# A two-layer graph attention kernel: its first stage laid out anew, and one carry in another form

## The reference

```python
xr = jnp.einsum('nd,rdf->rnf', x, W)
oi = xr[etype, dst]
oj = xr[etype, src]
alpha = jax.nn.leaky_relu(oi @ q + oj @ k, NEG_SLOPE)
m = jax.ops.segment_max(alpha, dst, num_segments=n_nodes)
e = jnp.exp(alpha - m[dst])
z = jax.ops.segment_sum(e, dst, num_segments=n_nodes)
a = e / (z[dst] + EPS)
msg = (a[:, :, None] * oj.reshape(-1, heads, out_ch)).reshape(-1, heads * out_ch)
out = jax.ops.segment_sum(msg, dst, num_segments=n_nodes) + b
# twice: h = elu(layer1(x)); x = layernorm(x + layer2(h))
```

## Time and profile before

| | us |
|---|---|
| median of 3 runs | 2490.14 (2489.93 to 2492.66) |
| the profiled execution | 2489.6 |
| its span, first to last instruction | 2488.0 |
| first stage (to the first dense product) | 122.97 |
| dense products of layer 1 (to the first edge step) | 575.75, to 698.72 |
| the rest | 1789.3 |

### The profile page before, as it was taken

One profiled execution on the slowest core, in us unless ns is written; L12 is line 12 of the kernel. 1 busy time (PEld: TensorE's weight loads), 2 busy tenths in 40 slices (PEclk: granted clock), 3 DMA queues, 4 the chain that ended last, 5 costly groups with the idle time before them and its releaser, 6 DMA issues.

```text
span 2488.0 us, 42686 instructions
## 1 busy us (share of the span) xinstructions
PE 2415.6 (97%) x10277; PEld 1677.5 (67%) x10277; DVE 1370.7 (55%) x2672; ACT 1051.6 (42%) x2973; POOL 1604.4 (64%) x1671
## 2 busy tenths in 40 slices
PE   6999999999989999999989999999997999999998
PEld 2755666666589999999976566665554555555554
DVE  8438566655588988888897443332331332333232
ACT  1111000000179999999975000000002566666664
POOL 1277777767367777777735766667723677777774
PEclk9899999999999999999999999999999999999999
DMA  8642333333279998989843222322226999999996
GB/s 298 192 128 61 89 102 104 101 78 78 61 272 328 322 315 309 326 308 326 301 163 106 69 85 82 92 81 75 75 62 181 340 336 348 334 340 344 340 332 236
DMA packets 164481, 505.17 MB, mean 203 GB/s; under 512 B 55800, under 2 KB 61473, under 8 KB 164132
## 3 DMA queue, kind: packets, MB, share of 16 engines
q0 software_dynamic: 95664, 354.41, 42.4%
q1 hardware_dynamic: 54449, 143.18, 17.8%
q10 hardware_dynamic: 14256, 6.14, 1.1%
HBM read 424.00 MB, written 79.54 MB: 202 GB/s over the span
## 4 chain that ended last, share of the span: by engine, by line
PE 91%; DMA 3%; POOL 2%; DVE 2%; issue 1%; DVEq 0%; ACT 0%; ACTq 0%; SPq 0%; POOLq 0%
PE banks L994 35%; PE banks L1036 23%; PE banks L1060 11%; PE banks L1056 11%; PE banks L879 3%; PE banks L710 3%; PE banks L902 1%; PE banks L897 1%; POOL q_fill L1435 1%; DMA big<-q_fill 1%; POOL big L1448 1%; PE banks L721 1%; PE banks L703 1%; POOL ring L1473 1%; DVE big L1649 1%
## 5 line engine op out<-in xcount | busy, mean ns | idle before, releaser
L1473 POOL DMA_INDIRECT ring<-xr_table,row_idx x704 | 666.7, 947 | 303.2 <-PE banks L1036 96.2
L1448 POOL DMA_INDIRECT big<-k_table,row_idx x700 | 683.1, 976 | 275.4 <-issue 203.6
L1252 ACT ACTIVATE work<-work,wE 128x125 f32<-128x125 f32 x1760 | 552.6, 388 | 36.7 <-DVE work L1954 22.4
L994 PE MATMUL banks<-work 128*125 128x384 f32 x1548 | 534.0, 488 | 0.0
L1036 PE MATMUL banks<-ring,work 128*125 128x193 f32 x2816 | 470.5, 327 | 7.6 <-DMA ring<-xr_table,row_idx 7.6
L1036 PEld LDWEIGHTS banks<-ring,work 128*125 128x125 f32 x2816 | 464.2, 187 | 7.8 <-issue 7.8
L1971 DVE TENSOR_TENSOR big<-big,banks 125x772 f32 x440 | 421.5, 958 | 64.9 <-PE banks L1036 57.7
L1825 DVE TENSOR_TENSOR ring<-ring,banks 125x384 f32<-125x384 f32 x330 | 182.2, 553 | 490.6 <-PE banks L994 489.2
L994 PEld LDWEIGHTS banks<-work 128*125 128x125 f32 x1548 | 283.4, 188 | 181.8 <-issue 0.6
L994 PE MATMUL banks<-big,work 128*125 128x384 f32 x1152 | 398.0, 487 | 0.0
L1274 ACT ACTIVATE work<-rel,wE 128x125 f32<-128x125 f32 x440 | 216.2, 491 | 234.5 <-PE banks L1060 225.4
(11 more groups left out here) (276 smaller groups left out, 2038.3 us busy)
## 6 DMA issues: line engine op xcount, KB each, us to landing
xr_table<-ring SPq DMA_DIRECT2D x75, 337.8 KB
xr_table<-ring SPq DMA_DIRECT2D x75, 336.9 KB
work<-in_L_gnn_W SPq DMA_DIRECT2D x36, 384.0 KB, 6.2
ring<-xr_table,row_idx POOLq DMA_INDIRECT x704, 5.0
big<-k_table,row_idx POOLq DMA_INDIRECT x700, 2.4
work<-in_x_turned SPq DMA_DIRECT2D x25, 375.0 KB, 5.3
out<-work SPq DMA_DIRECT2D x25, 336.0 KB
work<-in_x SPq DMA_DIRECT2D x23, 336.0 KB
```

The lines of the kernel that those rows point to most:

```text
L994: last = pe.matmul(bank[b][0:TN, 0:HALF], left_side(l, left, pair)[:, c, :], right_side(l, left, r)[:, c, :], start=(left in ("A11", "S1", ...
L1252: last = nc.scalar.activation(one_hots[l][:, slot, h, :], hot[:, slot, :], ACT.Copy, scale=wE[:, bass.ds(st, 1), h:h + 1].rearrange("p a b ...
L1448: nc.gpsimd.indirect_dma_start(k_at(l, st), None, ktab[l], bass.IndirectOffsetOnAxis(ap=row_idx[:, st:st + 1], axis=0)).then_inc(s["k_gath ...
L1473: nc.gpsimd.indirect_dma_start(row_slot(l, st % GS), None, xrtab[l], bass.IndirectOffsetOnAxis(ap=row_idx[:, st:st + 1], axis=0)).then_inc ...
```

## The change

1. **Loads.** q1 and k1 come as 24 contiguous numbers for each partition (`qk_rows`), and ACT copies them to `qkw`. Turned W1 is laid out to match, with 3 + 12 slots; the 12 new ones are the places in `work` where W1 of relations 2 and 1 goes later. SP no longer waits for slots until the 16th chunk. x tiles 0 to 9 come in between the last chunks, then tiles 20 to 24, W1 of relation 0, tiles 10 to 19, the rest of W1, and b1 last. The edge lists wait for 9 chunks on PE, the zero fill for two groups of x; it is read 12 times (3 for layer 2) from a 440-wide piece of `rel` that POOL clears.
2. **Counts.** Digits of 6 bits by shift and mask: 49 high, 64 low values. Ten rounds go with W1, seven with the first seven x groups. DVE's work on the edge lists stands behind the counts.
3. **x.** Tiles in 13 groups (`GROUPED`), ten of them pairs of tiles 0 to 19, then two, one and two. A pair is one product of 250 columns.
4. **Warming.** PE begins with 11 products of `iota_n` with itself.
5. **q carry of layer 1.** As in layer 2 before: one scan over `same` gives `q_first`, which is 1 up to the first change of node in a row, and the carry is a multiply-add on the scans already made. `sum_w(0)` stands between `q_ends` and `q_carries`.
6. **Spots.** The two turns of q move from units 3 and 4 of the third plain tile to units 0 and 2 of the fourth. The last `turn_k` and what follows it in the softmax stand later.

```diff
-    WSLOTS = 3
+    WSLOTS = 3 + 2 * DC
-    K_SPOTS = [[168, 171, 174, 186], [192, 194, 224, 227]]
-    ENDS_SPOT, CARRY_SPOT = [192, 230], [195, 233]
+    K_SPOTS = [[168, 171, 174, 193], [192, 194, 224, 227]]
+    ENDS_SPOT, CARRY_SPOT = [199, 230], [201, 233]
-    PASS_SPOTS = [[196, 198, 200, 202], [234]]
-    E_SPOTS = [[205, 207], [238]]
+    PASS_SPOTS = [[202, 203, 204, 205], [234]]
+    E_SPOTS = [[206, 208], [238]]
...
-            for n in range(WSLOTS):
+            for n in range(WT - ROOMS):
                 load_turned_w1(n)
+            for t in range(ROOMS):
+                load_turned_w1(WT - ROOMS + t)
+                load_room(t)
             for k in range(U):
-                load_turned_w1(WSLOTS + k)
...
+                    for c in range(DC):
+                        last = pe.matmul(out_, wsb[:, c, NQK - 2 * R * H:NQK], chunks[:, :, c, :],
+                                         start=(c == 0), stop=(c == DC - 1))
...
-                        if done < 3 * (n + 1) // 4:
+                        if n >= 2 and done < COUNTED_WITH_W * (n - 1) // (WT - 2):
...
+                    for u in range(FLATS):
+                        if done < HROUNDS:
+                            hist(done)
+                            done += 1
+                            if done == HROUNDS:
+                                hist_end()
+                        first_products(u)
+                        if u > 0:
+                            first_turn(u - 1)
+                        if u == COUNTS_AT + 3:
+                            turn_counts()
+                        if u == COUNTS_AT + 4:
+                            sum_counts()
+                    first_turn(FLATS - 1)
...
-                    meets = {0: {2: turn_rows}, 2: {3: turn_q_ends, 4: turn_q_carry}} if l == 0 else {}
+                    meets = {0: {2: turn_rows}, 3: {0: turn_q_ends, 2: turn_q_carry}} if l == 0 else {}
...
+                    for u in range(FLATS):
+                        if u == COUNTS_AT:
+                            act.wait_ge(cnt_ready, 1)
+                            act.dma_start(node_counts.rearrange("(a b) -> a b", a=HI), digit_counts).then_inc(counts_stored, 16)
+                        if u == COUNTS_AT + 1:
+                            act.wait_ge(counts_stored, 16)
+                            act.dma_start(counts, node_counts[0:N].rearrange("(t p) -> t p", p=TN)).then_inc(counts_loaded, 16)
+                        first_flat(u)
+                        if u > 0:
+                            first_nodes(u - 1)
...
             pool.wait_ge(pads_set, 1)
+            pool.wait_ge(LS[0]["qk_done"], 2 + WT // 2)
...
-            pool.wait_ge(zeros_set, 1)
+            pool.wait_ge(LS[0]["qk_done"], 2 + WT + 2)
...
                     for q in range(R * H):
-                        if l == 0:
-                            link(nc.vector.tensor_tensor_scan(qs[:, q, :], same[0:ROWS, :], raw[:, q, :], c_in[:, q:q + 1],
-                                                              ALU.mult, ALU.add))
-                        else:
-                            link(nc.vector.scalar_tensor_tensor(out=qs[:, q, :], in0=q_first, scalar=c_in[:, q:q + 1],
-                                                                in1=qs[:, q, :], op0=ALU.mult, op1=ALU.add))
+                        link(nc.vector.scalar_tensor_tensor(out=qs[:, q, :], in0=q_first, scalar=c_in[:, q:q + 1],
+                                                            in1=qs[:, q, :], op0=ALU.mult, op1=ALU.add))
```

253 lines of the change are left out of this document (130 added, 123 removed).

## The result

The changed kernel takes **2478.27 us** (median of 5 runs, 2475.89 to 2482.68) beside 2492.44 for the kernel before on the same chip (2489.93 to 2492.76): a ratio of 0.995, with a 95% interval of 0.9939 to 0.996. It is faster by some 14 us, as forecast in sign; the forecast was 2469 and its range 2460 to 2478. The median lies 0.3 us above that range and 9 above the forecast. The profiled execution took 2475.9 us, its span 2474.2.

What follows compares the result with a forecast made beforehand. PE, carrying 91% of the time to the end, bounds the kernel, so only an earlier start of its dense products pays: 20.5 + 0.7 = 21.2 us off the profiled 2489.6 gives 2468.4; median 0.5 higher, 2469, range 2460 to 2478.

Steps and rivals of the forecast that it cites:

- S: Time at which the count sums come in the first stage: forecast 91 us, 88.5 if the clock holds.
- the low clock between W1 and the groups: First stage: clock of 0.50 only near 47 to 53 us, for which 2.6 us were added.
- block products: Their start, behind the dense units and DVE's first x sums: 220.8 instead of 241.3, 20.5 us earlier; S + 129.8.
- The wait at the q ends: PE at the turn of the q ends: a 3.9 us wait where 0.3 stood, plus 1.4 for the clock.
- The carry: Layer 1's q carry on DVE by multiply-add: 0.77 us each, 9.2 instead of 15.8, 6.6 less.
- W1 is hidden behind DVE: First stage without slot gating: W1 chunks and ten x tiles land by 35 to 40 us, while DVE's tables set the pace.
- the forecast's own signs: Wrong if dense start lies past 102, the two-tile product isn't 2.6, or PE waits over 6 us in the dense stage.
- the counts' trip: Counts' round trip through HBM: 5.49 + 4.81 us, started at 75.4, back near 86, hidden with about 1 us of cover.
- Rival 2: First stage: counts' trip 3 to 5 us longer or rounds at 4 us, S 4 to 8 later: 2474 to 2478, chance 0.27.
- the first use of the tables: PE's first use of DVE's digit tables, after the fourth chunk of W1: near 13.5 us.
- the end of the dense stage: Last turn of k moved 7 products later: its 0.7 us wait goes; the 7.6 us to the first edge product stay.
- three gathers fewer: POOL's gathers beside DVE's new multiply-adds, 9 us: three fewer, 4 us of POOL, inside its pauses; sum unchanged.

Runs made afterwards that it cites:

- f1: The change with W1 of relations 2 and 1 held until the counts are back, ACT's table load ahead of q1 and k1, 17 warming products: 2469.93 us, ratio 0.9916.
- a0: The changed kernel run once more, nothing altered: 2480.61 us, ratio 0.9959 to the kernel before.
- a3: The change with layer 1's carry again by twelve scans, its output not the reference's: 2823.15 us beside 2843.7 for the kernel before, ratio 0.9917.
- f2: The kernel before with only layer 1's carry by multiply-add, second run: 2490.44 us, ratio 1.0001.
- e1: The change with SP again waiting on three W1 slots and PE waiting for each chunk by itself: 2485.58 us, ratio 0.9977.
- a1: The change with W1 of relations 1 and 2 and b1 held back until the counts are back: 2473.24 us, ratio 0.9933.
- a2: The change with the store of k of tiles 5 to 9 placed just behind the counts' store: 2479.88 us, ratio 0.9959.
- the ACT edit: ACT's digits copy, and with it its table load, moved ahead of its wait for q1 and k1; alone in the change, ratio 0.9939.
- g1: f1 with layer 1's spots as before the change: 2772.63 us beside 2787.0 for the kernel before, ratio 0.9947.
- b1: The change with ACT's digits copy and table load ahead of its wait for q1 and k1: 2831.3 us beside 2843.7 for the kernel before, ratio 0.9939.

## Why the prediction was right and wrong

**Right.** That an earlier start of the dense products is all that pays, and where the holes went. A group of a round, a pair and two turns takes 3.81 (3.9 forecast), a pair 2.64 (2.6), S to the dense start 5.3 (5.4), the low clock between W1 and the groups at 51 to 57 (47 to 53). From S on the chain came nearly as worked out: block products at S + 128.3 in the change and S + 128.8 in f1 (forecast S + 129.8). The 1.5 us are two small misses: the q ends were ready at S + 83.5 (84.2), and the 1.4 set aside for the clock behind them weren't spent, since it stayed at 1.00 from 181 to 190 us (in a0, after a wait of 3.19, it stood at 0.69 to 0.74 and the block products came at S + 130.6). The wait at the q ends was 2.2 instead of 3.9, in part because PE had already waited 1.0 at the turn of the edge rows, a wait that the forecast doesn't have. The carry took 9.42 (9.2), and a3 shows that it counted in full, f2 that it is worth nothing where PE comes later anyway. Taken back alone (e1), the slots are worth 5 to 7 us; the forecast had no price for them by themselves, only that W1 is hidden behind DVE with them gone; in the change no wait for W1 is left.

By the forecast's own signs it was wrong: the dense start lies past 102 (102.61), and PE waits over 6 us in the dense stage (1.0 + 2.2 + 1.4 + 1.4 + 0.3 = 6.3). The two-tile product is the 2.6.

**Wrong: the counts' trip.** The step read "started at 75.4, so the counts are back near 86 ... Cover of about 1 us". It took 15.65 us and PE stopped for 3.11 + 1.17. I had carried 5.49 + 4.81 over from the earlier trace rows, and that was the right price beside a full stream, which stood beside it there too; what I left out was the neighbour on its own queue. In the new order a store of k, 625 small pieces, is issued 1.0 us ahead of the counts (76.89 and 77.87), not 5.5 ahead (82.12 and 87.62). Rival 2 named the time (3 to 5 us longer) and gave the stream as its reason; a1 shows that the stream is needed, a2 that the neighbour is needed too. The stops are 4.3 of the 6.3 us by which S is late. Holding the stream back gave 5 to 7 us.

**Wrong: the first use of the tables.** 13.5 forecast, 15.94 and 16.91 measured, 13.76 to 14.03 where the clock was kept. I had let "the 11 warming products end near 6" and the first chunk begin by 8 or so without pricing the hole between them, although the forecast charges the clock behind every later hole. q1 and k1 landed at 7.4, then came ACT's table load of 1.28. Size: 2.4 us in the one profile, 3.4 in the other. Of the 2.4, some 0.9 are the later start of the first chunk (9.07, where 13.5 less four chunks of 1.34 makes 8.1) and 1.5 the clock (the four took 6.87 us, not 5.36); 2.0 of them were left at the last round. The rounds themselves kept their 3.5 us. Curing it gave the rest: 2473.2 to 2469.9, with the ACT edit, which alone brought no earlier first use.

**Wrong: the end of the dense stage.** The last turn of k waits no more (0.7, right), but the turn of the ends now waits 1.39 (its row stands above). It replaces that gain. What follows the first edge product is 1.3 us longer than in the profile of before (1790.6 against 1789.3); in f2, which changes nothing there, it is 1790.9, so that is no effect of the change but the difference between two profiles, as large as this.

**Was this the whole miss?** Nearly. f1, with both causes cured, gives 2469.93 against 2469 forecast, block products at 219.0 and the first edge product at 676.96 (forecast 220.8 and 677). That it comes within 1 us is in part luck, and no proof of every term: the start of the block products came 1.8 us better than forecast, the stretch to the first edge product 1.3 worse and what follows 1.5 worse. As for the chances: the case "2474 to 2478" stood at 0.27 and is the one that came, with S 6.3 us late (4 to 8 in that case) and half of its reason. A median 0.3 above its end means little beside executions from 2475.9 to 2482.7; what the case left out is the low clock behind the stop, 2.5 us in a0 and a2.

## What to carry to other kernels
Price a small transfer by its neighbours on its own queue, not only by the load of the DMA engines: a store of many small pieces 1 to 2 us ahead of it cost 4 to 5 us beside a full stream and nothing that shows without one. Warming products that end 2 to 3 us ahead of the first real one brought nothing; reaching up to it, and being more, they brought the tables' first use 2 to 3 us forward. A faster operation is worth what the engine that waits for it is late by: 6.5 us here, none there.

## What the runs showed of the hardware

**A DVE copy that lasts as long as POOL's memset.** In the change POOL's clearing of the sums and DVE's copy of four numbers ran together (POOL's row):

```profile
651.21 2.98 POOL L1498 MEMSET big<- 125x3456 f32 x1 [7.29 <-PE banks L1022]
```

and DVE's two copies of the same shape:

```profile
651.56 2.65 DVE L1893 COPY small<-big 110x4 f32<-110x4 f32 x1
654.25 0.17 DVE L1894 COPY small<-big 110x4 f32<-110x4 f32 x1
```

The first copy ended at 654.21 and the memset at 654.19; in f1 both moved 6.6 us earlier and the copy again took 2.66 and ended with the memset, at 647.6. In the kernel before and in g1, with the memset elsewhere, both copies took 0.17. This is the wait of 1.39 at the softmax ends. Not every DVE operation is held so: the same memset ran again at 666.90, and beside it two passes of line 1916, with two inputs in SBUF, took 1.53 as elsewhere. The Trainium skill (GPSIMD Engine Reference, Specifications) names contention of POOL with DVE instructions in a two-port mode or with two SBUF inputs; the rows show such a copy, with one input, held until the other engine was through. That the copy runs in such a mode, no run shows.

**Gathers beside DVE.** The average over all 700 gathers of k hides what DVE does to them: 976 ns in the kernel before, 979 in f2 with the multiply-adds, 983 in the change. Beside the multiply-adds one takes 1.27 us (in the change):

```profile
193.00 1.27 POOL L1485 DMA_INDIRECT big<-k_table,row_idx  x1 [0.30 <-issue]
```

That is six gathers at 1.27 to 1.33 (in f2 six at 1.24 to 1.27), where the scans of the kernel before left them at 1.02; beside the 110x2048 masks one takes 2.02 in all three, and alone 0.94. The forecast took 2.02 for the multiply-adds too ("three gathers fewer"), so it charged POOL too much; its sum counted neither.

**The same kernel on other chips.** On four other chips the kernel before takes 2787 to 2844 us instead of 2491. The first 105 us are the same within a few us there. Behind them b1's profile is longer than the change's by some 345 us, of which 138 are PE's own busy time (2549.4 against 2410.9 us; its granted clock is 0.91 to 0.95 from 105 to 700 us, where the change has 1.00 nearly throughout). The rest are waits, many with no releaser, first in the dense products while POOL gathers. One product each 2 to 3.5 us, in b1:

```profile
185.39 0.80 PE L907 MATMUL banks<-work 128*125 128x384 f32 x1 [2.70 <-issue]
```

What the engine waits for there, the trace doesn't show, and I don't know it. The 10 to 20 us of the change can be told on such a chip (ratios of 0.992 to 0.995 for the kernels with all of its parts), the worth of a part can't.
